# Every tile that TensorE reads starts on a 512-byte boundary of its partition; narrow tiles are gathered in front of them

## The reference, cut to what matters

```
x  = layernorm(x)                                  # no gain
# mixer, rows in sequences of 2048
p, gate = split(x @ W_in.T)                        # 512 -> 2 * 1024
u  = silu(conv4(p) + conv_b)                       # per channel
h  = scan(0.95 * h + 0.05 * (u @ W_B.T))           # 64 states
y  = (h @ W_C.T + D * u) * silu(gate)
a  = layernorm(y @ W_out.T + x) * g + b            # 1024 -> 512
# experts: each of 8 takes the 1024 rows with the highest gate
s  = (tanh(x @ gate_w.T) + 1) / 2
rows_e = top_k(s[:, e], 1024)
z  = layernorm(x[rows_e]) * g2 + b2
o  = (gelu(z @ fc1[e].T + b1) @ fc2[e].T + b2) * s[rows_e, e]
out = x + a + x.at[rows_e].add(o)
```

## Time and profile before

| | us |
|---|---|
| median of 3 runs | 2826.62 (2826.45 to 2827.22) |
| the profiled execution's own time | 2825.14 |
| its span | 2823.4 |
| TensorE matmul busy | 2758.5 (98% of the span), 12170 matmuls |
| TensorE weight loads busy | 2196.6 (78%) |
| VectorE, ScalarE, GpSimd busy | 1857.0, 1369.4, 686.2 |

### The profile page before, as it was taken

How to read it: one execution, slowest core, us unless ns; L and a number is a source line. 1 busy time by engine, 2 the same in 40 slices (tenths; PEclk the granted TensorE clock), 3 DMA queues, 4 the chain that set the end, 5 groups by cost and what they waited for, 6 DMA issues and landing times.

```text
span 2823.4 us, 40464 instructions
## 1 busy us (share of the span) xinstructions
PE 2758.5 (98%) x12170; PEld 2196.6 (78%) x12170; DVE 1857.0 (66%) x3098; ACT 1369.4 (49%) x2317; POOL 686.2 (24%) x1009
## 2 busy tenths in 40 slices
PE   7899999999999999999999999999999999999997
PEld 3578888888887777777788888888888888888886
DVE  8768888888877887788754555455554555455554
ACT  4644555455555555564544444444444444444443
POOL 4422222222222112124321122112221122112221
PEclk9999999999999999999999999999999999999999
DMA  9633323222223333326233042231422313314221
GB/s 348 241 119 105 97 82 97 90 89 95 91 96 97 105 105 105 105 75 199 80 83 83 16 127 54 69 87 26 113 69 47 104 32 100 82 23 121 39 46 16
DMA packets 118953, 265.11 MB, mean 94 GB/s; under 512 B 23968, under 2 KB 24160, under 8 KB 114784
## 3 DMA queue, kind: packets, MB, share of 16 engines
q1 hardware_dynamic: 84512, 164.83, 17.2%
q0 software_dynamic: 34240, 97.85, 14.8%
HBM read 208.86 MB, written 53.77 MB: 93 GB/s over the span
## 4 chain that ended last, share of the span: by engine, by line
PE 88%; DVE 6%; ACT 2%; issue 2%; DMA 1%; POOL 0%; DVEq 0%; ACTq 0%; POOLq 0%
PE po L1867 8%; PE po L1869 8%; PE po L1868 8%; PE ring L1458 8%; PE ring L1460 8%; PE ring L1459 8%; PE pb L1867 4%; PE pb L1869 4%; PE pb L1868 4%; PE pc L1869 4%; PE pc L1868 4%; PE pc L1867 4%; PE po L1491 3%; PE po L1493 3%; PE po L1492 3%
## 5 line engine op out<-in xcount | busy, mean ns | idle before, releaser
L1458 PE MATMUL ring<-xt_h,w_h 128*128 128x512 f32 x1024 | 402.6, 393 | 2.8 <-DVE xt_l L483 2.6
L1867 PE MATMUL po<-w2h,hid_h 128*128 128x512 f32 x1024 | 402.3, 393 | 1.0 <-DVE hid_l L1828 1.0
L1869 PE MATMUL po<-w2h,hid_l 128*128 128x512 f32 x1024 | 402.0, 393 | 0.0
L1868 PE MATMUL po<-w2l,hid_h 128*128 128x512 f32 x1024 | 401.9, 392 | 0.0
L1460 PE MATMUL ring<-xt_h,w_l 128*128 128x512 f32 x1024 | 401.0, 392 | 0.0
L1459 PE MATMUL ring<-xt_l,w_h 128*128 128x512 f32 x1024 | 398.7, 389 | 0.0
L1260 DVE SCALAR_TENSOR_TENSOR u<-xin,cw,u 128x512 f32<-128x512 f32 x384 | 288.5, 751 | 60.6 <-issue 28.7
L1795 ACT ACTIVATE hid<-pb,b1c 128x512 f32<-128x512 f32 x128 | 88.2, 689 | 410.7 <-PE pb L1869 410.7
L1718 POOL DMA_INDIRECT out_dram<-res,idx_c x64 | 101.3, 1583 | 738.5 <-DVE res L1854 724.2
L1828 DVE TENSOR_TENSOR hid_l<-hid,hid_h 128x512 fp32r<-128x512 f32 x128 | 88.7, 693 | 280.2 <-ACT hid_h L1799 280.2
L1828 DVE TENSOR_TENSOR hid_l<-xn_tail,hid_h 128x512 fp32r<-128x512 f32 x128 | 88.6, 692 | 241.8 <-ACT hid_h L1799 241.8
(11 more groups left out here) (207 smaller groups left out, 5959.9 us busy)
## 6 DMA issues: line engine op xcount, KB each, us to landing
wo<-wo_halves POOLq DMA_DIRECT2D x120, 512.0 KB, 4.0
w1r<-fc_in SPq DMA_DIRECT2D x130, 256.0 KB, 2.7
w2r<-fc_in SPq DMA_DIRECT2D x130, 256.0 KB, 3.0
g_x<-x_in SPq DMA_DIRECT2D x16, 1024.0 KB, 9.0
x_tail<-x_in SPq DMA_DIRECT2D x64, 256.0 KB, 2.7
out_dram<-res SPq DMA_DIRECT2D x64, 256.0 KB, 2.1
xt_rows<-g_xnt SPq DMA_DIRECT2D x15, 1024.0 KB, 10.6
rows<-xt_rows SPq DMA_DIRECT2D x15, 1024.0 KB, 5.9
```

The source lines that it names most:

```text
L1458: pe.matmul(ring[r % 2][:, :], w_h[:, r, q], xt_h[:, k, :], start=(k == 0), stop=False)
L1867: pe.matmul(dst, ah, bh, start=start, stop=False)
L1868: pe.matmul(dst, ah, bl, start=False, stop=False)
L1869: return pe.matmul(dst, al, bh, start=False, stop=stop)
```

## The change: what it does

Small tiles that TensorE doesn't read (or reads only a few columns of) are moved in front of the large ones, and fillers (`upto`, `line`) put the large ones on multiples of 512 bytes. `rows` loses the 8 columns of gathered gate values, which get a tile `row_gates` of their own; its rows are then 2048 bytes instead of 2080. The mixer's one-column and eight-column tiles (`carry`, `decay`, `step`, `cand`, `cnt`, `gain`, `total`, `one`, `row_no`) become slices of one tile `narrow`, and `ls.ones` becomes a part of `both`. No instruction of the loops is added, removed or moved; operands differ in address alone (and `keep` reads contiguous values instead of 8 out of every 520).

Start addresses modulo 512, worked out from the sizes in order:

| tile | read by TensorE as | before | after |
|---|---|---|---|
| `w_h`, `w_l` | stationary, mixer | 416 | 0 |
| `xt_h`, `xt_l` | moving, mixer and even expert groups | 416 | 0 |
| `u_h`, `u_l` / `wo` | stationary / moving, mixer | 416 / 416 | 0 / 0 |
| `wb`, `wc_hh`, `wc_lh` | stationary, `share_b` and `chan` | 320 | 0 |
| `h_hh`, `h_hl` | moving, `chan` | 160 | 0 |
| `w1h`, `w1l`, s % 4 = 0 and 2 | stationary, `hidden` | 320 | 0 |
| `w1h`, `w1l`, s % 4 = 1 and 3 | stationary, `hidden` | 0 | 0 |
| `yt_h1`, `yt_l1` | moving, odd expert groups | 0 | 0 |
| `w2h`, `w2l`, s % 4 = 2 / others | moving, `out_share` | 320 / 0 | 0 / 0 |
| `hid_h` | stationary, `out_share` | 0 | 0 |
| `hid_l`, s % 4 = 2 and 3 / others | stationary, `out_share` | 384 / 0 | 0 / 0 |
| `rows` / `ident` | transposes | 416 / 160 | 0 / 0 |
| `bis_cnt` (after: in `narrow`) / `l_both` | `tally` | 288 / 0 | 384 / 0 |
| `g_x`, `g_xnt` / `g_gw` / `g_sc_t` | gate stage | 0 / 352 / 224 | 0 / 352 / 0 |

The core of the diff:

```diff
+LINE = 512
+SB_END = 447 * LINE
 class Mem:
+    def upto(self, name, end):
+        gap = end - -(-self.nc.sbuf_base // 32) * 32
+        assert gap >= 0
+        if gap:
+            self.sb(name, [P, gap // 4])
+    def line(self, name):
+        self.upto(name, -(-self.nc.sbuf_base // LINE) * LINE)
 class Between:
+        self.narrow = m.sb("narrow", [P, 5 * E])
+        self.h_at = SB_END - 2 * TB * 4
 class MixerWeights:
+        self.before = m.sb("l_before", [P, P], BF16)
+        self.digit = m.sb("l_digit", [P, LO], BF16)
+        m.line("w_line")
 class Experts:
-        self.rows = m.sb("rows", [P, J, XW])
+        self.row_gates = m.sb("row_gates", [P, J, E])
+    def tiles(self, m):
+        self.w1 = m.sb("w_h", [P, NW, D], F32R)
...
+        self.rows = m.sb("rows", [P, J, D])
     def gather_gates(...)
-            out=self.rows[:, j, D:XW], ...
+            out=self.row_gates[:, j, :], ...
     def keep(...)
-        dve.tensor_copy(self.kept[i][:, :, :], self.rows[:, :, D:XW])
+        dve.tensor_copy(self.kept[i][:, :, :], self.row_gates[:, :, :])
 class Lists:
+    def tiles(self, m, narrow):
+        self.ones = self.both[:, 1, 0:P // 2].bitcast(BF16)
+        self.tile_no = m.sb("l_tile", [P, NT])
+        self.one, self.row_no = narrow[:, 3:4], narrow[:, 4:5]
+        self.total = narrow[:, 4 * E:5 * E]
 stage_mixer
+    carry, decay, step = (narrow[:, i:i + 1] for i in range(3))
+    cand, cnt, gain = (narrow[:, i * E:(i + 1) * E] for i in range(1, 4))
+    m.upto("m_gap", sums.h_at)
     h_hh = m.sb("h_hh", [P, TB], F32R)
 stage_experts
-    m.sb("f_gap", [P, 48])
+    m.sb("f_gap", [P, LINE // 4])
-    m.sb("f_gap2", [P, EXPERT_GAP])
     first = m.sb("f_first", [P, J, FT])
+    m.line("f_line")
     hid_l = hid_l + [m.sb(f"hid_l{i}", [P, TB], F32R) for i in range(2, 4)]
 build
+        thr = m.sb("threshold", [P, E])
-        gates = m.sb("gates", [P, E, NT])
-        thr = m.sb("threshold", [P, E])
-        ident = m.sb("ident", [P, P])
         ends = RowEnds(m, t, banks)
         ew = Experts(m, t, ends)
         sums = Between(m)
+        m.line("line")
+        gates = m.sb("gates", [P, E, NT])
+        ident = m.sb("ident", [P, P])
+        ends.tiles(m)
+        ew.tiles(m)
```

More of the change, by code:

```diff
@@ L116, in __init__ @@
         self.d_tick = m.tick("m_dtick")
+    def tiles(self, m):
+        self.x_rows = [m.sb(f"x_tail{j}", [P, D]) for j in range(J)]
+        self.xn_rows = [m.sb(f"xn_tail{j}", [P, D]) for j in range(J)]
+        self.xn_end = m.ends_at[f"xn_tail{J - 1}"]
+        self.res = [m.sb(f"res{j}", [P, D]) for j in range(J)]
+        self.gamma = m.sb("ln_g", [P, D])
+        self.beta = m.sb("ln_b", [P, D])
     def load_x(self, sp, b, j, first_turn=False):
@@ L586, in __init__, with tiles @@
         self.p_tick, self.d_tick = ends.p_tick, ends.d_tick
+    def tiles(self, m):
+        self.w1 = m.sb("w_h", [P, NW, D], F32R)
+        self.w2 = m.sb("w_l", [P, NW, D], F32R)
+        self.w1r = m.over("w1r", m.ends_at["w_h"], FT * D * 4, [P, FT, D])
+        self.w2r = m.over("w2r", m.ends_at["w_l"], FT * D * 4, [P, FT, D])
+        self.yt_h = [m.sb("xt_h", [P, KD, TB], F32R)]
+        self.yt_l = [m.sb("xt_l", [P, KD, TB], F32R)]
+        self.rows = m.sb("rows", [P, J, D])
+        self.gamma = m.sb("f_ln_g", [P, D])
+        self.beta = m.sb("f_ln_b", [P, D])
     def load(self, sp, e, i):
@@ L610, in gather_gates @@
         pool.indirect_dma_start(
-            out=self.rows[:, j, D:XW], out_offset=None, in_=self.t["gate_rows"][:, :],
+            out=self.row_gates[:, j, :], out_offset=None, in_=self.t["gate_rows"][:, :],
             in_offset=bass.IndirectOffsetOnAxis(ap=self.idx_c[i][:, j:j + 1], axis=0),
@@ L652, in keep @@
             dve.wait_ge(self.c_ga[j], 32 * (g + 1))
-        dve.tensor_copy(self.kept[i][:, :, :], self.rows[:, :, D:XW]).then_inc(self.c_kp, 1)
+        dve.tensor_copy(self.kept[i][:, :, :], self.row_gates[:, :, :]).then_inc(self.c_kp, 1)
 ROUNDS = 3
@@ L688, in __init__ @@
         self.token = m.over("l_token", m.ends_at["l_lo1_1"], TQ * E * LO * 2, [P, 2, LO], U32)
[L689 to L695, removed]
+        self.before, self.digit = w.before, w.digit
         self.hi1 = [x[:, :].rearrange("p (t e l) -> p t e l", t=TQ, e=E) for x in (self.gt, self.eq)]
@@ L878, in stage_mixer @@
     h = xin[0][:, 0:TB]
+    narrow = sums.narrow
+    carry, decay, step = (narrow[:, i:i + 1] for i in range(3))
+    cand, cnt, gain = (narrow[:, i * E:(i + 1) * E] for i in range(1, 4))
+    ls.tiles(m, narrow)
+    ge = ls.by_expert(ls.gt[:, :])
+    m.upto("m_gap", sums.h_at)
     h_hh = m.sb("h_hh", [P, TB], F32R)
     h_hl = m.sb("h_hl", [P, TB], F32R)
[L881 to L887, removed]
     ones = ls.both[:, 0, 0:P]
@@ L1513, in tally @@
             pe.wait_ge(c_cnt, n + 1 + 1)
-            pe.matmul(sums_at[:, 0:E], ones, cnt[:, :], start=True, stop=True).then_inc(c_tot, 1)
+            pe.matmul(sums_at[:, 0:E], ones, cnt, start=True, stop=True).then_inc(c_tot, 1)
         def bisect_0(c):
@@ L1532, in prefix @@
                 pe.wait_ge(ls.c_mask, 1 + 1)
-                pe.matmul(pb[:, :], ls.ones[:, :], ls.gt[:, :], start=True, stop=True).then_inc(ls.c_pre, 1)
+                pe.matmul(pb[:, :], ls.ones, ls.gt[:, :], start=True, stop=True).then_inc(ls.c_pre, 1)
             if c == 4:
@@ L1540, in slots @@
                 pe.wait_ge(ls.c_mask, 2 + 1)
-                pe.matmul(pb[:, :], ls.ones[:, :], ls.eq[:, :], start=True, stop=True).then_inc(ls.c_pre, 1)
+                pe.matmul(pb[:, :], ls.ones, ls.eq[:, :], start=True, stop=True).then_inc(ls.c_pre, 1)
             if c == 4:
```

73 lines of the change are left out of this document (28 added, 45 removed).

## The result

| | before | after |
|---|---|---|
| median of the runs | 2826.53 (2823.99 to 2827.22) | 2796.20 (2795.68 to 2796.34) |
| ratio after / before | | 0.9895, 95% interval 0.9884 to 0.9907 |
| profiled execution: own time | 2825.14 | 2796.34 |
| its span | 2823.4 | 2794.6 |

The changed kernel is 1.05% faster, about 30 us. The forecast was 2793.0 with a range of 2786 to 2807. The profiled executions differ by 28.8 us; the sum made against them was -33.5.

What follows compares the result with a forecast made beforehand. TensorE, busy 98% of the span, bounds the kernel through its matmuls' start-to-start cost. Experts -25.5 and mixer -8.0 sum to -33.5 us from 2825.14, giving 2791.6; with the median 1.5 higher, 2793, range 2786 to 2807.

Steps and rivals of the forecast that it cites:

- What costs is that the two operands of neighbouring work differ modulo 512.: Wide matmuls: differing residues cost 234 ns start to start in step 4 of `hidden`, against 226.7 in the quick stretch.
- Experts, -25.5: Expert stage: 28.4 us excess over 8 pairs of groups, less 2.9 left; bounds 15.4 to 28.4 us saved.
- a tenth stays: Expert stage: a tenth of the excess, 2.9 us, remains as slower matmuls after restarts, no matter of address.
- Mixer, -8.0: Mixer: 10.5 us from `share_b` and `chan` pairs, partly lost to waits; bounds 0 to 10.5 us saved.
- The 41 ns: Mixer: each of 256 `share_b` or `chan` pairs costs 0.041 us extra, its entry and wake, 10.5 us in all.
- I let half of it go: Mixer: six of 16 pairs, from `chan` 2 on, hold 3.9 us; half is lost to TensorE's waits.
- another 0.5 for the blocks that build the lists: Mixer: a further 0.5 us of the saving is lost in the list-building blocks.
- TensorE's waits for `y_low` a few us above 23.6.: Mixer `out_share`, a sign of the forecast: TensorE's waits for VectorE grow a few us from 23.6.
- Transposes, gate stage, `keep`, narrow tiles: 0.: These parts change nothing; bounds 2 us either way for transposes, and 2 us for `keep` and narrow tiles.
- Rival 1: Whole kernel: addresses don't matter, the excess belongs to something that goes along with them; 2826.6 us, no change; 5%.
- Rival 2: VectorE takes back more: mixer gives nothing, experts their lower half; 2801 to 2811 us; 10%.
- Rival 3: All engines in step: VectorE and ScalarE accesses meet TensorE's, matmuls cost 234 ns; +46 us, 2872; 4%.

Runs made afterwards that it cites:

- the three fillers: Kernel before with three expert-stage fillers resized by 96, 64 and -128 bytes, so its wide TensorE tiles stand at 160 modulo 256, mixer untouched: 2803.1 us, ratio 0.9916.
- the second profile of the changed kernel: The changed kernel run again with no edit, on one chip beside the residue-416 kernel: 2794.51 us, ratio 0.9889.
- the second experiment: Changed kernel with the mixer's `wb`, `wc_hh` and `wc_lh` put back to 192 modulo 512, moving tiles still at 0: 2799.25 us, ratio 0.9905.

## Why the prediction was right, and where it wasn't

- **"What costs is that the two operands of neighbouring work differ modulo 512."** Right that it is the difference; wrong modulus. It is 256. `yt` at 256 keeps the odd groups at 2.72. The sum didn't depend on it, and that was luck: no two neighbouring wide tiles of the kernel before stood 256 apart. That nothing else changed the time is shown for the experts, by the three fillers. In the mixer it is argued: moving the small weights back to 192 brings 4.1 us back, but no run had the old differences there with the new tiles.
- **Experts, -25.5: measured -24.2.** The price of 0.08 us per `hidden` read off held over the groups (0.075 to 0.09), and the excess taken from the group lengths was within 1 us. Counted over all distances up to 262 ns, the excess over 226.7 ns went from 27.5 to 2.9 us: "a tenth stays" held, while the excess itself, 28.4 from one pair of groups, was 0.9 too large for the eight; longer waits grew from 7.9 to 8.3. These two are the whole 1.3 us. What stays stands behind something. In the timeline after, behind four transposes of group 5, with every residue equal:

```profile
1851.06 0.60 PE L1895 MATMUL ring<-ident,rows 128*128 128x128 f32 x4
1851.41 0.48 PE L1886 MATMUL pb<-yt_h,w1h 128*128 128x512 f32 x1
1851.73 0.39 PE L1887 MATMUL pb<-yt_l,w1h 128*128 128x512 f32 x1
```

The first matmul takes 0.32 us to the next, the following five 0.23 to 0.24 before the pace is back at 0.227. The prediction was right to keep this apart from the address.

- **Mixer, -8.0: measured -6.7 at full clock, -5.0 in the profiled execution.** The 41 ns hold for the `share_b` pairs: they went from 463 to 453 ns and the step behind from 2.75 to 2.72, 40 ns together. The `chan` pairs stand among waits, and by the second profile of the changed kernel their median saving, the 12 matmuls behind included, was 27 ns. "I let half of it go" for the six pairs behind `chan` 2 was near the mark in the ordinary blocks: 16 x 0.041 = 0.66 us saved, 0.50 kept (75.0 to 74.5 in blocks 1 to 8). The mis-sized term is "another 0.5 for the blocks that build the lists". The four blocks 11 to 14 keep 0.2 us each instead of the 0.53 that the sum gave a block, 1.3 us less in all, and blocks 0, 1 and 15 keep 0.4 each, another 0.4 less. In block 12 the step behind `chan` 0 (started at 1068.84 after, 1073.24 before) has to wait for ScalarE. Before, TensorE and ScalarE:

```profile
1073.24 0.39 PE L1478 MATMUL pc<-h_hh,wc_hh 128*128 128x512 f32 x1
...
1073.91 0.51 PE L1458 MATMUL ring<-xt_h,w_h 128*128 128x512 f32 x1
...
1072.49 0.89 ACT L814 ACTIVATE l_run_eq<-l_lo,l_tile 128x256 bf16<-128x256 bf16 x2
1073.29 1.05 ACT L1147 ACTIVATE sg<-ring 128x512 f32<-128x512 f32 x2
```

and after:

```profile
1068.84 0.39 PE L1497 MATMUL pc<-h_hh,wc_hh 128*128 128x512 f32 x1
...
1069.68 0.50 PE L1477 MATMUL ring<-xt_h,w_h 128*128 128x512 f32 x1 [0.22 <-ACT sg L1166]
...
1068.25 0.89 ACT L834 ACTIVATE l_run_eq<-l_lo,l_tile 128x256 bf16<-128x256 bf16 x2
1069.05 1.05 ACT L1166 ACTIVATE sg<-ring 128x512 f32<-128x512 f32 x2
```

ScalarE works without a gap from `h_hh` and `h_hl` (which follow VectorE's scan) through `x_tail` and its share of the lists to `sg`. The next step starts 0.62 us after `sg` does, before (1073.29 to 1073.91) and after (1069.05 to 1069.68). `sg` starts 0.05 us behind that `chan` before and 0.21 after: TensorE is 0.16 us earlier against that row of work, and from `chan` 0 to the next step it takes 0.84 instead of 0.67 us (its two matmuls alone are 0.45). The chance that something takes the gain back was priced on VectorE alone; here it was ScalarE, in four blocks: the waits between 980 and 1300 us after have the row below, and before there was none of its kind.

```profile
PE ring L1477 <- ACT sg L1166: 0.9, 4, 0.2
```

- **"TensorE's waits for `y_low` a few us above 23.6."** Not so: 22.9. What the mixer's distances over 262 ns take beyond 226.7 each did grow, from 40.6 to 43.3 us, but 1.6 us of that is the slow clock at the mixer's start. In the second profile of the changed kernel, without it, they take 41.7: growth of 1.1 us, in several small places, among them the 0.9 us for ScalarE. In that profile the excess of the distances up to 262 ns went from 10.2 to 2.5 us; the two together are the 6.7.
- **Transposes, gate stage, `keep`, narrow tiles: 0.** Nothing seen; transposes start 108 to 109 ns apart in both kernels. By the modulus found here no change was due: `ident` at 160 and `rows` at 416 are 256 apart and agreed already, which the prediction, counting by 512, took for a difference. The kernel before with three fillers has the same expert stage without any of these edits.
- **The clock** was in no term: 1.6 us in the profiled execution. In the profiles of this study it fell to 0.57 to 0.63 at this place in seven of twelve, always behind the same 2.6 us in which TensorE idles; kernels with quite different addresses are on either side.
- **Rival 1 (addresses don't matter)** is refuted by moving single tiles: 2.72 against 2.79 for one and the same step with `yt` at 0 and at 128. **Rival 2** (2801 to 2811) asked for a mixer that gives nothing; it gave 5.0 and 6.7 us. **Rival 3** (all in step, slower) is refuted twice: with all tiles at 0 and with all at 416 every step that isn't next to transposes or a wait stands at 2.72.
- The Trainium skill ("SBUF — State Buffer", "Who interferes with whom" and "Operand start alignment") has TensorE's two reads independent of each other, and of alignment it says that its rule "is about legality, not speed" and that its runs timed nothing. So the second section is silent on speed, and it is the first by which one would expect no price. The measurement disagrees with that: 2.72 against 2.75 to 2.81 us per 12 fp32 matmuls, by nothing but a start address that is legal in both cases. The measurement decides.

## What to carry to other kernels

Where TensorE is busy throughout, measure matmuls from start to start, not by their duration, and compare like steps whose operands lie at different places. Then put the stationary and the moving tiles of neighbouring matmuls at one residue modulo 256, whichever it is (shown here for float32 alone); three fillers were enough for three quarters of this gain. A saving of nanoseconds per matmul is kept whole where TensorE alone sets the pace (the experts), and partly given back wherever another engine's row of work ends just in time.

## What the runs showed of the hardware that I had not expected

- With 128 x 128 weight loads beside 128 x 512 matmuls in float32, 226.7 ns from start to start if moving tile, its own weights and the weights loaded under it agree modulo 256; 229 to 234 ns on average of 12 if they don't (single distances go from 224 to 240). A difference of 32 bytes costs as much as one of 128; one of 192 half. Why is open: the runs show that, not what in the memory or its ports makes it. Differences under 32 bytes were not tried.
- After a pause or short matmuls the first wide matmul takes some 0.32 to 0.34 us to the next, and the following five to ten mostly take 229 to 236 ns, with all residues equal and the clock at 1.00. The runs give no cause.
- The granted clock fell at the mixer's start, after 2.6 us without a matmul, in 7 of 12 profiles, to 0.57 to 0.63 on average over 4 us, with six to eight matmuls some 0.43 us apart. That is the lower of its two levels (1.2 GHz) for 512 columns. While matmuls ran it fell once more in every profile, to 0.50 behind a wait in which two matmuls start 1.9 us apart (at 191 us in the kernel before, at 860 us in the second experiment), and stayed at 1.00 behind four like waits of the same mixer. What decides between the two outcomes is open.
